# Weight sums one per slot, loaded two slots ahead, with their low parts on VectorE, in a fused attention and feed-forward kernel

## The chip, the cores and the metric

One core of a Trainium2 chip runs the whole program in one launch. The metric is the time of one execution on the device in microseconds. The engines named here are TensorE (PE in the profile), VectorE (DVE), ScalarE (ACT), GpSimd (POOL) and SyncE (SP), whose queue issues all the DMAs. Each engine runs its instructions in the order in which they are written, and engines wait for each other by semaphores.

## What is computed

The input x is 2 x 1024 x 512 in float32. A causal linear attention with 16 heads and its output projection are added to x, and then a gated feed-forward part:

```python
x = x + _layernorm(_L0_attn_ref(_layernorm(x), Wq, Wk, Wv, Wo))
x = x + _layernorm(_L0_ffn_ref(_layernorm(x), w_gate, w_up, w_down))

def _L0_ffn_ref(x, w_gate, w_up, w_down):
    h = silu(x @ w_gate) * (x @ w_up)      # 512 -> 2048
    h_sparse = _sparsify_2to4(h)           # of each 4 neighbours the 2 largest by size stay
    return h_sparse @ w_down               # 2048 -> 512
```

## The kernel before

Every large product is made of three fast multiplications. Each operand is split into a high part (ScalarE's cast to the short format fp32r) and a low part (the value less its high part), and high x high, low x high and high x low are added up in a bank. The profile shows the three as lines 784, 785 and 786. So every weight is loaded raw, cast by ScalarE, and its low part is made by another engine: in this kernel mostly GpSimd, whose helper `lo` is line 1906 for all of them.

The work is laid out in ticks. Attention takes slots a0 to a65. The feed-forward part takes slots f0 to f75; a slot here means one of these, `slot_f(n)`, of which each engine has its own. f0 stands between a64 and a65. Slots 0 to 31 handle the first batch row: slot n has a gate projection and an up projection of 12 multiplications each, and from slot 6 on one down projection of 12 for the hidden rows made earlier. From slot 32 on the second batch row is handled with fewer products, from sums of weight blocks (the manner of Strassen). For these the kernel makes, during slots 1 to 17, 16 **rounds of weight sums**, and keeps them in HBM (`s_keep`).

Round r goes through these steps:

- `load_sums(r)` on SyncE, line 595: two DMAs of 256 KB bring raw weights into one of four buffers of the tile `x_part`. It waits until the earlier round of that buffer is stored.
- `sum_weights(r)` on VectorE, lines 1642 to 1647: four additions or subtractions over 128x256 elements, in place, at the end of slot `SUM_AT[r]`.
- `split_sums(r)` on ScalarE, line 1285: the high part, 128x1024, into `x_hi`, in slot `SUM_AT[r] + 1`, behind ScalarE's weight splits of that slot (line 1187).
- `sum_low(r)` on GpSimd, line 1906 with `x_lo<-x_part`: the low part, 128x1024, over the raw sums, in slot `SUM_AT[r] + 1`, behind GpSimd's weight splits of that slot.
- `store_sums(r)` on SyncE, line 601: two DMAs of 512 KB, in slot `SUM_AT[r] + 2`.

Rounds 0 to 3 are loaded just before the feed-forward slots, the later ones at slot `max(SUM_AT[r-4] + 3, SUM_AT[r] - 2)`, at the end of what SyncE does in the slot. With the numbers of before, the store rule is the larger for most rounds: loads stand in SyncE's queue one slot ahead of their sum (round 4: load in slot 4, sum in slot 5). In front of them in a slot stand that slot's loads of `x_rows` (line 573), weight pieces (line 558, each waits until GpSimd has split the piece four before it), stores of split weights (`w_keep`, line 628) and stores of sums.

The rest of a slot that matters here:

- VectorE starts slot n with the gate product (line 1755: up projection of slot n-1 times its gated value). TensorE's up projection of slot n waits for that product of slot n-1 (`dve_h >= n - 1`). In slots with n % 4 == 3 comes the first comparison pair (lines 1602 to 1604), with n % 4 == 0 the second one and `keep_two` (lines 1609 to 1630), which masks four hidden rows. In every slot from 6 on one down projection is accumulated (1736, 1738). Behind these come variances of rows (1465) and last the sums.
- The masked rows are cast by ScalarE (1359). GpSimd makes the low parts of the first two (1906, `big_lo`) ahead of its weight splits of the slot, VectorE those of the other two at the start of the next slot (`first_lows`, 1635). The first down projection of these rows stands in TensorE's slot two later (6, 10, 14, 18, 22) behind the gate projection, and it needs all four low parts and the last split "down" weights of the unit, which are split in slot 4, 13, 21 and 29.
- From slot 19 on rows of the second batch row are turned (837) and split into `x_hi` and `x_lo`, over the buffers of the sums; ScalarE waits there until the stores of the sums have landed.

Of the kernel before, what the change touches and what calls it, by code (L numbers as in the profile page):

```python
# [8 lines left out]
ALU = mybir.AluOpType  # L9
ACT = mybir.ActivationFunctionType  # L10
F32 = mybir.dt.float32
# [24 lines left out]
ROUNDS = 4 * NU  # L36
# [12 lines left out]
def tick_f(n):  # L49
    return 65 if n == 0 else 66 + n  # L50
# [42 lines left out]

SUM_AT = [1, 2, 2, 3, 5, 6, 6, 7, 9, 10, 10, 11, 13, 14, 14, 15]


def sum_place(r):
    return 2 + r // 2 % 2, r % 2  # L100


def sum_buffer(r):
    half, a = sum_place(r)
    return 2 * (3 - half) + a
# [125 lines left out]
def pieces_at(tick, kinds):  # L231
    return [k for k, (piece, when) in enumerate(PLAN) if when == tick and piece[0] in kinds]
# [19 lines left out]
def build(nc, x, wq, wk, wv, wo, wg, wu, wd, cos_t, sin_t, causal, eye, x1, v_rest, s_keep, w_keep, out):  # L252
    with ExitStack() as ctx:
# [10 lines left out]
        def sem(name):  # L264
            return ctx.enter_context(nc.semaphore(name))
# [105 lines left out]
        def sum_raw(r):  # L371
            half, a = sum_place(r)
            return part[:, half, 2 * a:2 * a + 2, :]

        def sum_split(r):
            half, a = sum_place(r)
            return Xh[:, half, 2 * a:2 * a + 2, :], Xl[:, half, 2 * a:2 * a + 2, :]
# [96 lines left out]
        pe_g, pe_u, pe_d = sem("pe_g"), sem("pe_u"), sem("pe_d")  # L474
        ld_s = [sem(f"ld_s{i}") for i in range(4)]
        st_s = [sem(f"st_s{i}") for i in range(4)]
        dve_s1, dve_ss, act_ss, pool_ss = [sem(n) for n in ("dve_s1", "dve_ss", "act_ss", "pool_ss")]
        dve_t, act_t, pool_t = sem("dve_t"), sem("act_t"), sem("pool_t")
        ld_r = [sem(f"ld_r{i}") for i in range(RING)]
        st_k = [sem(f"st_k{i}") for i in range(8)]  # L480
# [67 lines left out]
        def _(sp):  # L548
            g = Gate(sp)
# [37 lines left out]
            def load_sums(r):  # L587
                k, up, buffer = r // 2, r % 2, sum_buffer(r)
                g.wait_ge(pe_q, 4 * STEPS)
                g.wait_ge(pe_k, STEPS)  # L590
                g.wait_ge(pe_v, B * TT)
                g.wait_ge(st_s[buffer], 32 * sum_uses(r))
                to = sum_raw(r).rearrange("p j (i c) -> p j i c", i=2)
                for i in range(2):
                    sp.dma_start(to[:, :, i, :], (wu if up else wg)[k // 2, 2 * (k % 2) + i].rearrange(
                        "p (j c) -> p j c", j=2)).then_inc(ld_s[buffer], 16)

            def store_sums(r):
                g.wait_ge(pool_ss, r + 1)
                for n, of in enumerate(sum_split(r)):  # L600
                    sp.dma_start(s_keep[r, n].rearrange("j p w -> p j w"), of.bitcast(F32)).then_inc(st_s[sum_buffer(r)], 16)

# [107 lines left out]
            for kind, i in TICKS:  # L710
# [44 lines left out]
                for r in range(4):  # L755
                    if tick == tick_f(0) - 2 + SUM_AT[r]:
                        load_sums(r)
                if kind == "f":
                    for r in range(ROUNDS):
                        if SUM_AT[r] + 2 == i:  # L760
                            store_sums(r)
                    for r in range(4, ROUNDS):
                        if max(SUM_AT[r - 4] + 3, SUM_AT[r] - 2) == i:
                            load_sums(r)
# [379 lines left out]
        def _(act):  # L1144
# [137 lines left out]
            def split_sums(r):  # L1282
                g.wait_ge(dve_ss, r + 1)
                g.wait_ge(st_s[sum_buffer(r)], 32 * sum_uses(r))
                copy(sum_split(r)[0], sum_raw(r)).then_inc(act_ss, 1)
# [47 lines left out]
            def slot_f(n):  # L1333
# [29 lines left out]
                for r in range(ROUNDS):  # L1363
                    if SUM_AT[r] + 1 == n:
                        split_sums(r)
# [82 lines left out]
        def _(dve):  # L1448
            g = Gate(dve)
# [188 lines left out]
            def sum_weights(r):  # L1638
                two, three = [sum_raw(r)[:, 0, half] for half in HALVES]
                four, one = [sum_raw(r)[:, 1, half] for half in HALVES]  # L1640
                g.wait_ge(ld_s[sum_buffer(r)], 32 * (sum_uses(r) + 1))
                dve.tensor_tensor(one, three, one, ALU.add).then_inc(dve_s1, 1)
                dve.tensor_tensor(three, two, three, ALU.subtract)
                g.wait_ge(dve_s1, 2 * r + 1)
                dve.tensor_tensor(two, one, two, ALU.subtract).then_inc(dve_s1, 1)
                g.wait_ge(dve_s1, 2 * r + 2)
                dve.tensor_tensor(four, four, two, ALU.subtract).then_inc(dve_ss, 1)

            def combine_x(step):
                high = [block[0].bitcast(F32) for block in (B11, B21, B12, B22)]  # L1650
                low = [block[1].bitcast(F32) for block in (B11, B21, B12, B22)]
                b11, b21, b12, b22 = range(4)
                if step == 0:
                    g.wait_ge(dve_xl, len(TURNS))
                    g.wait_ge(pe_u, EDGE - 4)
                if step == 6:
                    g.wait_ge(pool_wl, len(PLAN))
                g.wait_ge(dve_t, (0, 0, 1, 2, 3, 4, 5, 7, 8, 9)[step])
                to, first, other, op = ((raw_t1, high[b12], high[b11], ALU.subtract),
                                        (raw_t3, high[b22], high[b12], ALU.subtract),  # L1660
                                        (raw_t1, raw_t1, low[b12], ALU.add), (raw_t3, raw_t3, low[b22], ALU.add),
                                        (raw_t1, raw_t1, low[b11], ALU.subtract),
                                        (raw_t3, raw_t3, low[b12], ALU.subtract),
                                        (raw_t2, high[b22], raw_t1, ALU.subtract), (raw_t2, raw_t2, low[b22], ALU.add),
                                        (raw_t4, high[b21], raw_t2, ALU.subtract),
                                        (raw_t4, raw_t4, low[b21], ALU.add))[step]
                dve.tensor_tensor(to, first, other, op).then_inc(dve_t, 1)
# [77 lines left out]
            def slot_f(n):  # L1745
# [91 lines left out]
                for job in stats:  # L1837
                    variance(job)
                for r in range(ROUNDS):
                    if SUM_AT[r] == n:  # L1840
                        sum_weights(r)
                for step in {28: (0, 1), 29: (2, 3, 4), 30: (5, 6), 31: (7,)}.get(n, ()):
# [59 lines left out]
        def _(pool):  # L1902
            g = Gate(pool)

            def lo(dst, full, hi):
                return pool.tensor_tensor(dst, full, hi.bitcast(F32), ALU.subtract)  # L1906
# [47 lines left out]
                for job in at(tick, add_tick, ADDS):  # L1954
                    add(job)

            def sum_low(r):
                g.wait_ge(act_ss, r + 1)
                lo(sum_split(r)[1], sum_raw(r), sum_split(r)[0]).then_inc(pool_ss, 1)

            def t_low(n):
                to, of, count = ((T1, raw_t1, 7), (T3, raw_t3, 6), (T2, raw_t2, 8), (T4, raw_t4, 10))[n]
                g.wait_ge(act_t, n + 1)
# [13 lines left out]
            def slot_f(n):  # L1977
                tick = tick_f(n)
                for k in pieces_at(tick, "d"):
                    if not last_down(PLAN[k][0]):  # L1980
                        split(k)
                for job in at(tick, norm_tick, LATER):
                    scaling(job)
                if n == EDGE:
                    t_low(2)
                if n % 4 == 0 and 4 <= n <= EDGE:
                    d = n // 4 - 1
                    for i in range(2):
                        g.wait_ge(act_hh, 4 * d + i + 1)
                        lo(hidden(d)[1][:, i, :], hid[:, i, :], hidden(d)[0][:, i, :]).then_inc(pool_hl, 1)  # L1990
                for k in pieces_at(tick, "gud"):
                    if not last_down(PLAN[k][0]) and PLAN[k][0][0] == "d":
                        continue
                    split(k)
                for r in range(ROUNDS):
                    if SUM_AT[r] + 1 == n:
                        sum_low(r)
                if n in (30, 31):
                    t_low(n - 30)
                if n == EDGE + 2:  # L2000
                    t_low(3)
                if EDGE <= n < SLOTS:
                    k, beat = quad_of(n)
                    v, late = k // 2, k % 2
                    if beat == 1 and v:
                        hidden_lows(2 * (NU + v - 1) + late)
                if n == SLOTS:
                    hidden_lows(STEPS - 2)
                if n == SLOTS + 2:
                    hidden_lows(STEPS - 1)  # L2010
                for u in DOWN_AT:
                    for i in range(4):
                        if DOWN_AT[u][i] == n:
                            split_down(u, i)
                for job in at(tick, norm_tick, ENDING[:-1]):
                    scaling(job)
                for job in at(tick, norm_tick, ENDING[-1:]):
                    g.wait_ge(act_nm, len(SCALED) - 4)
                    deviation(job)
                for job in at(tick, add_tick, ADDS[:-4]):  # L2020
                    add(job)
# [69 lines left out]
```

## Time and profile before

| | us |
|---|---|
| median of 3 runs | 1245.32 (1244.94 to 1245.99) |
| profiled execution | 1244.29 |
| its span | 1242.5 |
| TensorE busy | 1185.8 (95%) |
| VectorE busy | 858.3 (69%) |
| ScalarE busy | 520.7 (42%) |
| GpSimd busy | 510.2 (41%) |

Busy is the time in which at least one instruction of the engine was running. A TensorE that is busy may still run at a lower clock; the page has a row for the clock that was granted. Feed-forward slots 1 to 21 take the time from about 663 to 877 us of the span. An idle time in square brackets behind a row is the one just before the instruction, with what ended it.

### The profile page before, as it was taken

To read this page: it belongs to the slowest core of one execution; us is meant where nothing else is said; L and a number is where in the kernel's file an instruction comes from. 1 tells how busy PE (TensorE), PEld (TensorE's weight loads), DVE (VectorE), ACT (ScalarE), POOL (GpSimd) and SP (SyncE) were. 2 spreads that over 40 slices of the span, in tenths; PEclk is the share of its full clock that TensorE was granted. 3 is DMA by queue.
4 is the path that set the end of the run, shared out by engine and by line. 5 is a ranking of instruction groups with operands and counts; after the bars stand their busy time and mean duration, and the time that the engine had idled before them with its cause. 6 is when DMAs were issued, how large, how long until landed. Compare 5 with 4: busy or idle time off the path is not lost.

```text
span 1242.5 us, 16278 instructions
## 1 busy us (share of the span) xinstructions
PE 1185.8 (95%) x5862; PEld 990.2 (80%) x5862; DVE 858.3 (69%) x1412; ACT 520.7 (42%) x1017; POOL 510.2 (41%) x397
## 2 busy tenths in 40 slices
PE   9999999999999999999999777799999999999987
PEld 7888888888888888888888565577787787888865
DVE  8845665666755466665656684876669869768698
ACT  4533544445444344454455232333432444334332
POOL 5512524425553143351555544554435633112124
PEclk9999999999999999999999998899999999999998
DMA  6321423314532233232365458456422565343411
GB/s 216 90 68 43 128 53 88 86 41 108 140 116 83 64 96 85 62 96 52 102 184 185 164 191 290 146 182 229 136 82 88 172 218 186 119 153 119 153 68 69
DMA packets 96368, 153.78 MB, mean 124 GB/s; under 512 B 10272, under 2 KB 31008, under 8 KB 96288
## 3 DMA queue, kind: packets, MB, share of 16 engines
q1 hardware_dynamic: 96288, 152.74, 39.5%
q8 instruction: 47, 0.77, 0.2%
q14 instruction: 33, 0.27, 0.1%
HBM read 96.60 MB, written 40.89 MB: 111 GB/s over the span
## 4 chain that ended last, share of the span: by engine, by line
PE 69%; DVE 16%; POOL 4%; issue 3%; DMA 3%; SPq 2%; ACT 2%; DVEq 0%; ACTq 0%; POOLq 0%
PE bank_q L786 7%; PE bank_q L784 7%; PE bank_q L785 7%; PE bank_y L786 5%; PE bank_y L785 5%; PE bank_y L784 5%; PE bank_od L1011 5%; PE bank_od L1014 4%; PE bank_t L784 3%; PE bank_t L786 2%; PE bank_t L785 2%; PE bank_s L908 2%; POOL big_lo L1906 2%; DMA x_part<-wu 2%; PE bank_s L784 2%
## 5 line engine op out<-in xcount | busy, mean ns | idle before, releaser
L784 PE MATMUL bank_q<-x_hi,w_hi 128*128 128x512 f32 x464 | 187.6, 404 | 0.5 <-ACT scratch L1313 0.4
L786 PE MATMUL bank_q<-x_lo,w_hi 128*128 128x512 f32 x464 | 182.7, 394 | 0.0
L785 PE MATMUL bank_q<-x_hi,w_lo 128*128 128x512 f32 x464 | 182.1, 393 | 0.0
L1906 POOL TENSOR_TENSOR w_lo<-stage,w_hi 128x512 fp32r<-128x512 f32 x60 | 78.6, 1319 | 127.0 <-ACT w_hi L1187 126.3
L1906 POOL TENSOR_TENSOR big_lo<-q_rows,big_hi 128x1024 fp32r<-128x1024 f32 x31 | 74.0, 2386 | 116.9 <-ACT big_hi L1226 116.9
L786 PEld LDWEIGHTS bank_q<-x_lo,w_hi 128*128 128x128 f32 x464 | 87.8, 189 | 19.2
L784 PEld LDWEIGHTS bank_q<-x_hi,w_hi 128*128 128x128 f32 x464 | 88.1, 190 | 18.6 <-ACT scratch L1313 1.5
L785 PEld LDWEIGHTS bank_q<-x_hi,w_lo 128*128 128x128 f32 x464 | 88.3, 190 | 16.8
L786 PE MATMUL bank_y<-wout_lo,a_hi 128*128 128x512 f32 x256 | 100.0, 391 | 0.0
L784 PE MATMUL bank_y<-wout_hi,a_hi 128*128 128x512 f32 x256 | 99.8, 390 | 0.0
L785 PE MATMUL bank_y<-wout_hi,a_lo 128*128 128x512 f32 x256 | 99.8, 390 | 0.0
L1906 POOL TENSOR_TENSOR big_lo<-hidden,big_hi 128x512 fp32r<-128x512 f32 x24 | 48.7, 2046 | 123.1 <-ACT big_hi L1359 75.6
L1011 PE MATMUL bank_od<-v_rows,scratch 128*128 128x130 f32 x512 | 95.1, 275 | 0.0
L1255 ACT ACTIVATE scratch<-bank_od,small 128x128 f32<-128x128 f32 x256 | 73.2, 373 | 42.2 <-DVE small L1555 42.2
L1014 PE MATMUL bank_od<-st_rows,q_rows 128*128 128x130 f32 x448 | 86.6, 275 | 0.0
L1267 ACT CAST a_hi<-bank_s 128x512 fp32r<-128x512 f32 x64 | 37.5, 586 | 111.0 <-PE bank_s L908 111.0
L1011 PEld LDWEIGHTS bank_od<-v_rows,scratch 128*128 128x128 f32 x512 | 79.1, 191 | 3.7
L1906 POOL TENSOR_TENSOR wout_lo<-stage,wout_hi 128x512 fp32r<-128x512 f32 x42 | 66.8, 1612 | 34.0 <-ACT wout_hi L1187 34.0
L1344 ACT ACTIVATE scratch<-hidden 128x512 f32<-128x512 f32 x32 | 20.3, 633 | 122.5 <-DVE hidden L1755 122.5
L1911 POOL TENSOR_TENSOR small<-small 128x1 f32<-128x1 f32 x64 | 38.4, 600 | 73.8 <-DVE small L1469 73.6
L1014 PEld LDWEIGHTS bank_od<-st_rows,q_rows 128*128 128x128 f32 x448 | 67.5, 190 | 0.0
L1587 DVE TENSOR_TENSOR a_lo<-bank_s,a_hi 128x512 fp32r<-128x512 f32 x64 | 44.2, 691 | 25.2 <-ACT a_hi L1267 25.1
(418 smaller groups left out, 3112.0 us busy)
## 6 DMA issues: line engine op xcount, KB each, us to landing
q_rows<-scratch SPq DMA_DIRECT2D x116, 128.0 KB, 2.3
x_rows<-x SPq DMA_DIRECT2D x48, 256.0 KB, 3.0
stage<-wq SPq DMA_DIRECT2D x32, 256.0 KB, 2.7
stage<-wo SPq DMA_DIRECT2D x32, 256.0 KB, 2.7
s_keep<-x_hi SPq DMA_DIRECT2D x16, 512.0 KB, 4.3
s_keep<-x_lo SPq DMA_DIRECT2D x16, 512.0 KB, 5.3
w_hi<-s_keep SPq DMA_DIRECT2D x32, 256.0 KB, 3.0
w_lo<-s_keep SPq DMA_DIRECT2D x32, 256.0 KB, 4.1
```

The source lines that it names most:

```text
L784: pe.matmul(ps, whi, xhi, start=first, stop=False, skip_group_check=True)
L785: pe.matmul(ps, wlo, xhi, start=False, stop=False, skip_group_check=True)
L786: return pe.matmul(ps, whi, xlo, start=False, stop=last, skip_group_check=True)
L908: ins = pe.transpose(psS[:, h * P:(h + 1) * P], Tn[:, h * P:(h + 1) * P], ident[:, :])
L1011: ins = pe.matmul(o, Sf[:, h * P:(h + 1) * P], Vr[:, c, :], start=True, stop=first, skip_group_check=True)
L1014: ins = pe.matmul(o, Q[:, (2 * p + h // 2) % 4, h % 2, t], St[:, :], start=False, stop=True, skip_group_check=True)
L1255: act.activation(Tn[:, h * P:(h + 1) * P], sums[:, h // 2, h % 2, 0:P], ACT.Identity, scale=share[:, h:h + 1]).then_inc(act_a, 1)
L1267: copy(Ah[:, :, :].rearrange("p h t -> p (h t)"), psS[:, :]).then_inc(act_ah, 1)
L1344: act.activation(ab[:, i, :], hid[:, i, :], ACT.Abs).then_inc(act_ab, 1)
L1587: dve.tensor_tensor(Al[:, :, :].rearrange("p h t -> p (h t)"), psS[:, :], Ah[:, :, :].rearrange("p h t -> p (h t)").bitcast(F32), ALU.subt ...
L1906: return pool.tensor_tensor(dst, full, hi.bitcast(F32), ALU.subtract)
L1911: pool.tensor_tensor(rstd[q % 4], mv[q % 4][:, 1:2], mhalf, ALU.pow).then_inc(pool_rs, 1)
```

## The change

`SUM_AT` becomes strictly increasing, one sum per slot, in slots 0 to 19 instead of 1 to 15. By the rule above, the loads of rounds 4 to 15 go to slots 3, 4, 5, 7, 8, 9, 11, 12, 13, 15, 16, 17: each two slots ahead of its sum. Round 0's load stands at tick a63 (was a64) and its sum in slot f0. The low part moves from GpSimd to VectorE, where it stands in slot `SUM_AT[r] + 1` ahead of that slot's own sum. The store waits for VectorE's semaphore.

```diff
-SUM_AT = [1, 2, 2, 3, 5, 6, 6, 7, 9, 10, 10, 11, 13, 14, 14, 15]
+SUM_AT = [0, 1, 2, 3, 5, 6, 7, 9, 10, 11, 13, 14, 15, 17, 18, 19]
...
             def store_sums(r):
-                g.wait_ge(pool_ss, r + 1)
+                g.wait_ge(dve_sl, r + 1)
...
+            def sum_low(r):
+                high, low = sum_split(r)
+                g.wait_ge(act_ss, r + 1)
+                dve.tensor_tensor(low, sum_raw(r), high.bitcast(F32), ALU.subtract).then_inc(dve_sl, 1)
...
                 for job in stats:
                     variance(job)
                 for r in range(ROUNDS):
+                    if SUM_AT[r] + 1 == n:
+                        sum_low(r)
+                for r in range(ROUNDS):
                     if SUM_AT[r] == n:
                         sum_weights(r)
...
-            def sum_low(r):
-                g.wait_ge(act_ss, r + 1)
-                lo(sum_split(r)[1], sum_raw(r), sum_split(r)[0]).then_inc(pool_ss, 1)
...
-                for r in range(ROUNDS):
-                    if SUM_AT[r] + 1 == n:
-                        sum_low(r)
```

## Rows read from the trace of the kernel before

**Rows 1.** Stretches: us, busy of PE, PEld, DVE, ACT, POOL (xcount), PEclk, DMA, GB/s.
```profile
663.00:880.00 217.00, 183.44 (x735) 144.13 (x734) 151.36 (x234) 73.83 (x120) 113.42 (x73) 0.91 0.59 199
880.00:960.00 80.00, 80.00 (x363) 65.97 (x362) 57.66 (x91) 28.28 (x48) 32.99 (x24) 1.00 0.33 109
...
765.00:772.00 7.00, 6.02 (x15) 4.80 (x16) 2.19 (x5) 2.57 (x4) 3.61 (x2) 0.54 1.00 338
```

**Rows 2.** Waits of TensorE, 663 to 880: us in total, times, longest.
```profile
PE bank_t L784 <- DVE hidden L1755: 11.7, 4, 5.8
PE bank_od L784 <- POOL big_lo L1906: 5.2, 2, 5.0
```

**Rows 3.** Waits of VectorE in the same stretch.
```profile
DVE x_part L1642 <- DMA x_part<-wg: 22.4, 2, 12.7
DVE x_part L1642 <- DMA x_part<-wu: 17.4, 5, 6.6
DVE small L1465 <- DMA x_rows<-x: 11.3, 2, 9.7
```

**Rows 4.** Chain of waits, 745 to 770: start us, us, what.
```profile
743.41 4.12 POOL big_lo L1906 x2
...
748.79 1.69 POOL u_lo L1906
...
757.14 1.33 SPq L595
...
765.15 6.08 DMA x_part<-wu
```

**Rows 5.** Instructions of tile x_part: duration ns min/median/max, first and last start.
```profile
L1906 POOL TENSOR_TENSOR x_lo<-x_part,x_hi x18: 2367/2570/2854, 678.7 to 958.8; 128x1024 fp32r<-128x1024 f32 x18
...
L1642 DVE TENSOR_TENSOR x_part<-x_part x16: 417/426/2527, 666.4 to 818.4; 128x256 f32<-128x256 f32 x16
...
L1643 DVE TENSOR_TENSOR x_part<-x_part x16: 412/420/2606, 667.8 to 818.8; 128x256 f32<-128x256 f32 x16
...
L1285 ACT CAST x_hi<-x_part x16: 1034/1042/1057, 672.7 to 837.1; 128x1024 fp32r<-128x1024 f32 x16
L1667 DVE TENSOR_TENSOR x_part<-x_part,x_lo x4: 1214/1216/2319, 945.2 to 952.0; 128x1024 f32<-128x1024 f32 x4
...
DMA to landing us min/median/max: 3.1/5.2/6.7
```

**Rows 6.** Tile x_part by stretch: us, busy of DVE, ACT, POOL, PEclk, DMA, GB/s.
```profile
663.00:880.00 217.00, 51.26 (x64) 16.31 (x16) 41.31 (x16) 0.91 0.59 199
```

**Rows 7.** VectorE in order of time: start us, us, line, operation, tiles.
```profile
699.97 0.69 DVE L1755 TENSOR_TENSOR hidden<-bank_q,scratch 128x512 f32<-128x512 f32 x1 [1.26 <-POOL big_lo L1906]
...
713.12 0.43 DVE L1642 TENSOR_TENSOR x_part<-x_part 128x256 f32<-128x256 f32 x1 [9.79 <-DMA x_part<-wg]
...
714.59 0.68 DVE L1755 TENSOR_TENSOR hidden<-bank_t,scratch 128x512 f32<-128x512 f32 x1
...
734.94 0.68 DVE L1755 TENSOR_TENSOR hidden<-bank_t,scratch 128x512 f32<-128x512 f32 x1
...
744.48 0.68 DVE L1630 TENSOR_TENSOR hidden<-hidden,scratch 128x512 f32<-128x512 f32 x1
746.43 0.69 DVE L1755 TENSOR_TENSOR hidden<-bank_q,scratch 128x512 f32<-128x512 f32 x1 [1.26 <-POOL big_lo L1906]
...
794.65 0.69 DVE L1755 TENSOR_TENSOR hidden<-bank_q,scratch 128x512 f32<-128x512 f32 x1 [1.26 <-POOL big_lo L1906]
...
836.82 0.69 DVE L1755 TENSOR_TENSOR hidden<-bank_q,scratch 128x512 f32<-128x512 f32 x1 [1.29 <-POOL big_lo L1906]
...
871.67 0.69 DVE L1755 TENSOR_TENSOR hidden<-bank_q,scratch 128x512 f32<-128x512 f32 x1 [0.26 <-POOL big_lo L1906]
```

**Rows 8.** ScalarE's high parts of rounds 4 and 7, in order of time.
```profile
717.36 1.04 ACT L1285 CAST x_hi<-x_part 128x1024 fp32r<-128x1024 f32 x1
...
746.76 1.04 ACT L1285 CAST x_hi<-x_part 128x1024 fp32r<-128x1024 f32 x1
```

More of the change, by code:

```diff
@@ L476, in build @@
         st_s = [sem(f"st_s{i}") for i in range(4)]
-        dve_s1, dve_ss, act_ss, pool_ss = [sem(n) for n in ("dve_s1", "dve_ss", "act_ss", "pool_ss")]
+        dve_s1, dve_ss, act_ss, dve_sl = [sem(n) for n in ("dve_s1", "dve_ss", "act_ss", "dve_sl")]
         dve_t, act_t, pool_t = sem("dve_t"), sem("act_t"), sem("pool_t")
```

## The prediction

> **What bounds the kernel now.** I read first the busy time by stretch. In the 217 us from 663 to 880 TensorE issued 735 multiplications at a granted clock of 0.91; in the 80 us after it, which run the same slots, 363 at 1.00 [rows 1]. At that later rate 735 need 162 us, so about 55 us of this stretch are lost, part as gaps and part as slow clock: in a piece right behind a long gap the granted clock reads 0.54 [rows 1]. The rest of the kernel is not touched by the change, except where a store of this stretch is waited for later. All rounds of weight sums lie in slots 1 to 17, which is this stretch.
>
> Next, who makes TensorE wait. There are two kinds, each the longest of its sort in [rows 2]: the "up" projection of slot n waits for VectorE's gate product of the slot before (line 1755, 11.7 us in 4 waits), and the first down projection of each group of four waits for the hidden rows' low parts (5.2 us in 2, and three more places of the kind). Both are VectorE running late: its in-order stream holds the masks in slots 4, 8, 12 and so on, the products, and the sums at the end of a slot. VectorE in turn waits 39.8 us for the raw weights that the sums read, in 7 waits of up to 12.7 us, and 11.3 us for rows of x [rows 3]. The third view, the chain of waits over slots 8 to 10, says why those loads are late [rows 4]: GpSimd's hidden low parts, then its weight splits, the sums' low part, then SyncE's stores, and only then the load at 757.1, landed 7 us later.
>
> Beside the waits VectorE is slowed. A sum operation over 128x256 takes 0.42 us at its least and median but up to 2.61 us [rows 5]; the long ones lie beside GpSimd's 128x1024 low part of 2.4 to 2.9 us. All 64 of them took 51.3 us, GpSimd's 16 low parts 41.3 [rows 6]. Undisturbed, a round passes in 1.5 us (from 713.12 to the next product at 714.59) [rows 7], 24 us in all. So some 27 us of VectorE are contention.
>
> The pace is read from VectorE's products that open slots 5, 9, 13, 17 and 21: 699.97, 746.43, 794.65, 836.82, 871.67 [rows 7]. The distances are 46.5, 48.2, 42.2 and 34.9 us, 171.7 together. Four slots of TensorE are 144 multiplications, 31.7 us at 363 per 80 us; some of these 363 are short transposes, so I take 32.7.
>
> **Part 1, sums one per slot, loads two slots ahead.** No round of work is added: 16 sums and 32 loads stay, spread over slots 0 to 19 in place of 1 to 15. A load now stands one slot earlier in SyncE's queue relative to its sum, so it has one slot (8 us) more; the worst wait was 12.7. I walk slot 8, the worst one. The last mask product ends at 745.2 (call it K) [rows 7]. In SyncE's queue of slot 8 come two weight loads which wait for GpSimd's splits behind the hidden low parts, then four stores of split weights, then the stores of the sums (one round now, two before), then load 8. It was issued at K+12.0 [rows 4]. With one round of stores less (2 DMAs; a DMA's issue took 1.33 us there [rows 4]) and without the sum's low part in GpSimd's queue (2.8 us, partly behind others) it goes at K+10 and lands at K+17. VectorE now wants it in slot 10, after its own slot 9, the low part and the product of slot 10, which I put at K+13.5 (wait for ScalarE 2.6, low part 1.2, slot 9's 4.7, slot 10's product and accumulation 1.2, wait 2.6, low part 1.2): a wait of 3.5 us where there were 12.7. Load 5, behind slot 4 where fewer commands stand, and loads 6 and 9 come out within 0 to 1 us of their sums; those of slots 3, 7, 11 to 13 land well ahead. So of 39.8 us some 5 stay (bounds 0 and 20, the latter if SyncE's queue is not relieved at all and each load in a quad's first slot is 6 us late). Round 0 now sums before the last attention slot's VectorE work; that stood idle for TensorE there, and it costs nothing unless the load issued some 5 us earlier lands over 2 us late.
>
> **Part 2, low parts from GpSimd to VectorE.** Removed from GpSimd: 16 operations of 2.58 us, 41.3 us [rows 6], and with them the 27 us of contention in the sums. Added to VectorE: 16 operations; the same shape, two inputs in SBUF, takes it 1.22 us at its least and median [rows 5], 19.5 us in all, all of it in the stream that sets the pace. The rows leave two prices open.
> The new wait: a low part waits for ScalarE's high part (1.04 us), and the next sum, the next slot's gate product and through it TensorE's next "up" stand behind it. In a mask slot the cast ended at 747.80, 2.6 us behind the last mask product; in another slot it began 2.8 us behind the gate product (714.59 to 717.36) [rows 7, 8] and ended at 3.8, of which the product and one accumulation cover 1.2, or 3.0 with the first comparisons. So a wait of 2.6, 2.6 and 0.8 us, 6 us per four slots; bounds 0 (GpSimd's and VectorE's other work hides it) and 9 (ScalarE late on weights).
> The contention that is left: GpSimd keeps the weight splits (one of 1.69 us stands in [rows 4]) and the hidden low parts (4.12 for a pair). I take 2.5 us per four slots, a split and a half met at its full length; bounds 0 and 8, four of its operations and more.
> What the trace shows of this contention is a VectorE operation of 0.42 us lasting 2.61 beside one of GpSimd. The Trainium skill, SBUF — State Buffer, section "SBUF: two separate sides", says the two share a port pair as an exclusive lock, held for the whole instruction, against VectorE operations with two SBUF inputs; the 2.61 agrees. Its Perfetto Trace Analysis, section "Optimizing Scalar/DVE Operations", draws from this that moving work between the two "might not help": that speaks against part 2 and is the third rival below.
>
> **The sum.** VectorE's work per four slots, undisturbed: from the gate product of a mask slot to the last mask product 10.2 us (734.94 to 745.2) [rows 7]; the other three slots' products, accumulations, comparisons and low parts 6.7 (eleven operations of 0.6); three sums 4.5; three low parts 3.6. That is 25. With 6 for ScalarE and 2.5 for contention: 33.5, close to TensorE's 32.7. The four distances become: slots 5 to 9, 33; 9 to 13, 37 (the 3.5 us wait of round 8); 13 to 17, 35; 17 to 21, 37 (a wait of up to 8 us for rows of x stays as the 11.3 of today, and low parts and sums of rounds 13 to 15 are new there). Together 142 against 171.7: 29.7. Before slot 5 the early sums, whose operations meet GpSimd's two low parts in slot 4, end about 4 us earlier (3 to 6). TensorE then regains another 1 us of clock. 34.5 us in all; the profiled run took 1244.3 (span 1242.5), the median is 1245.3, one more, and I add it: about 1210. Of the 55 us lost, 20 stay: a first down projection in slot 6 about 2 us late, slot 10 two, slot 14 six or seven (the last down weights are split behind the late gate product), slot 21 and 22 six, with clock after each. Errors of the walk, slot by slot, are worth 10 us either way: 1199 to 1220.
>
> **Rivals.**
> 1. The loads stay late: SyncE's queue waits as now for GpSimd's splits, the waits of mask slots stay, and the distances are 40, 40, 38 and 38 (today's less half the gain): 156 against 171.7 and 4 before, 1225. For it: the longest waits begin behind GpSimd, whose order keeps the splits behind the hidden low parts. Against: the extra slot.
> 2. TensorE alone sets the end: the ScalarE waits fall into slack, 5 us of loss stay, 1194.
> 3. The port makes the two engines one: what GpSimd stops doing VectorE does, and its sums still meet the remaining splits. Then only the load waits go (35) less 19.5 of low parts; 15 to 20 of these reach TensorE: about 1226. For it the 2.61 us; against it that one operation costs VectorE 1.22 and GpSimd 2.58, and that the largest GpSimd operations are those that go.
> 4. Slower: the queues close a ring. VectorE's low part waits for ScalarE's cast, which stands behind weight splits, whose loads stand in SyncE's queue behind the store that now waits for that low part. If the ring closes within one slot, a slot takes low part 1.2, store and load issue 2.5, landing 5.2 (to 6.7) [rows 5], split 0.6, cast 1.0 and wait 0.8: 11.3 to 12.8 us where the average now is 10.7 (171.7 over 16). That loses 10 to 33 us: 1265. It decides when a weight piece is loaded less than one slot before its split; the plan has most of them two slots ahead, and so I give it little.
> 5. One gain eats the other: VectorE loses in low parts and waits what it wins, 1245.
>
> **How the numbers follow.** Forecast 0.64, rival 1 0.12, rival 2 0.06, rival 3 0.10, rival 4 0.05, rival 5 0.03. The predicted time is the forecast's, 1210. From 1198 to 1226 lie the forecast with both errors and rivals 1 and 3; outside lie 2, 4 and 5. Faster by over 0.2% (about what a measurement can tell here) is 0.92, within it 0.03, slower 0.05.
>
> **What would show it.** The x_part waits of VectorE fall from 39.8 to about 5 us; the four sum operations have a mean near 0.45 us; sixteen x_lo operations of 1.2 to 2.5 us stand on VectorE, with about 25 us of waits for x_hi; TensorE's wait on line 1755 goes from 11.7 to under 2; the granted clock of the stretch is over 0.95; slot 21's product comes 33 us earlier, near 839. If that product comes as early but the end does not, something after slot 22 is wrong; if the low parts last 2.5 us each, rival 3 holds; if waits on x_hi are over 50 us, rival 4.

## The result, and the profile after

The changed kernel takes 1216.08 us (median of 4 runs, 1214.53 to 1218.87) against 1245.13 before in the same comparison; the ratio is 0.9771, with an interval of 0.9748 to 0.9794. By the ratio that is 28.5 us less (29.1 by the two medians, 27.1 in the spans of the two profiled executions, 1242.5 and 1215.4), where 35 were forecast.

The stretches of the changed kernel, with the columns of [rows 1]: the slots that took 217 us now take 190, and the 80 us behind them run as before.

```profile
663.00:853.00 190.00, 174.74 (x732) 141.15 (x731) 148.62 (x249) 73.88 (x121) 80.30 (x58) 0.95 0.65 219
853.00:933.00 80.00, 80.00 (x363) 65.99 (x362) 56.80 (x90) 27.59 (x48) 32.18 (x24) 1.00 0.37 122
```

At 363 per 80 us, 732 multiplications need 161 us, so 29 are lost where 55 were. The granted clock rose from 0.91 to 0.95. Next, who waits for whom in this stretch, first TensorE, then VectorE (rows 2 and 3 of before):

```profile
PE bank_st L837 <- DVE x_lo L1484: 7.3, 2, 4.5
PE bank_od L784 <- DVE big_lo L1635: 2.9, 3, 1.1
PE bank_od L784 <- issue: 2.5, 1, 2.5
PE bank_y L784 <- POOL wout_lo L1914: 2.3, 1, 2.3
```

```profile
DVE x_lo L1652 <- ACT x_hi L1285: 21.4, 12, 2.7
DVE small L1465 <- DMA x_rows<-x: 6.9, 1, 6.9
...
DVE x_part L1642 <- DMA x_part<-wg: 1.6, 1, 1.6
DVE x_part L1642 <- DMA x_part<-wu: 1.2, 1, 1.2
```

TensorE's wait for the gate product, 11.7 us in [rows 2], is gone. VectorE's wait for raw weights fell from 39.8 us [rows 3] to 2.8. The new wait for the high part is 21.4 us. What the operations of the sums cost VectorE, by line (busy us, mean ns, idle before and its cause); line 1652 is the low part that moved:

```profile
L1652 DVE TENSOR_TENSOR x_lo<-x_part,x_hi 128x1024 fp32r<-128x1024 f32 x16 | 26.3, 1641 | 21.4 <-ACT x_hi L1285 21.4
L1643 DVE TENSOR_TENSOR x_part<-x_part 128x256 f32<-128x256 f32 x16 | 11.0, 688 | 0.0
L1645 DVE TENSOR_TENSOR x_part<-x_part 128x256 f32<-128x256 f32 x16 | 9.9, 617 | 0.0
L1642 DVE TENSOR_TENSOR x_part<-x_part 128x256 f32<-128x256 f32 x16 | 9.7, 608 | 2.7 <-DMA x_part<-wg 1.6 <-DMA x_part<-wu 1.2
L1647 DVE TENSOR_TENSOR x_part<-x_part 128x256 f32<-128x256 f32 x16 | 7.7, 484 | 0.6
```

By the durations of their rows the four sum operations fell from 54 us to 38.3. Undisturbed, 64 operations of 0.42 us would be 27, so of 27 us of contention with GpSimd some 11 stay. And the pace, by the products that open slots 5, 9, 13, 17 and 21, as in [rows 7]:

```profile
698.83 0.68 DVE L1760 TENSOR_TENSOR hidden<-bank_q,scratch 128x512 f32<-128x512 f32 x1
...
734.48 0.68 DVE L1760 TENSOR_TENSOR hidden<-bank_q,scratch 128x512 f32<-128x512 f32 x1
...
768.08 0.68 DVE L1760 TENSOR_TENSOR hidden<-bank_q,scratch 128x512 f32<-128x512 f32 x1
...
805.75 0.68 DVE L1760 TENSOR_TENSOR hidden<-bank_q,scratch 128x512 f32<-128x512 f32 x1
...
844.78 0.68 DVE L1760 TENSOR_TENSOR hidden<-bank_q,scratch 128x512 f32<-128x512 f32 x1
```

The distances are 35.7, 33.6, 37.7 and 39.0 us: 146.0 together, where they were 171.7. Slot 21's product comes 26.9 us earlier, and so does all that follows. VectorE's own balance over just this part, slots 5 to 21, says what the 25.7 us are. The first fence is of before, the second of the changed kernel:

```profile
699.97:871.67 171.70, 145.26 (x572) 113.23 (x572) 115.57 (x180) 54.70 (x89) 85.73 (x52) 0.90 0.61 210
```

```profile
698.83:844.78 145.95, 134.84 (x568) 108.75 (x566) 115.36 (x193) 53.98 (x88) 58.20 (x39) 0.96 0.67 229
```

VectorE is as busy as it was, 115.6 and 115.4 us: what it won in contention it spent on the low parts. Its idle time fell from 56.1 to 30.6 us, by 25.5, and that is the gain. Within it the waits for raw weights fell by 34.4 us, from 37.2 to 2.8, and 14.7 us of waits for the high part are new. Which of the two parts of the change brought what can't be read from this balance; experiment 1 has them apart.

### The profile page after: what moved, and what is told of

It is laid out like the page before. It is cut to its first block, busy times and chain, and to the rows that moved or that the text cites. A ratio compares the mean times of both kernels' runs of the same rounds, so it can differ in the third digit from the quotient of the medians.

```text
span 1215.4 us, 16278 instructions
## 1 busy us (share of the span) xinstructions
PE 1176.5 (97%) x5862; PEld 986.5 (81%) x5862; DVE 857.9 (71%) x1428; ACT 521.0 (43%) x1017; POOL 476.1 (39%) x381
## 4 chain that ended last, share of the span: by engine, by line
PE 74%; DVE 14%; ACT 3%; issue 3%; POOL 3%; SPq 2%; DMA 2%; DVEq 0%; ACTq 0%
PE bank_q L784 8%; PE bank_q L786 8%; PE bank_q L785 8%; PE bank_y L784 5%; PE bank_y L786 5%; PE bank_y L785 5%; PE bank_od L1011 5%; PE bank_od L1014 4%; PE bank_t L784 3%; PE bank_t L786 3%; PE bank_t L785 3%; PE bank_s L908 2%; PE bank_s L784 2%; PE bank_s L785 2%; PE bank_s L786 2%
## 5 line engine op out<-in xcount | busy, mean ns | idle before, releaser
L1267 ACT CAST a_hi<-bank_s 128x512 fp32r<-128x512 f32 x64 | 37.6, 587 | 109.7 <-PE bank_s L908 109.7
L1919 POOL TENSOR_TENSOR small<-small 128x1 f32<-128x1 f32 x64 | 41.5, 648 | 75.3 <-DVE small L1469 74.9
```

The source lines that it names most:

```text
L1267: copy(Ah[:, :, :].rearrange("p h t -> p (h t)"), psS[:, :]).then_inc(act_ah, 1)
L1919: pool.tensor_tensor(rstd[q % 4], mv[q % 4][:, 1:2], mhalf, ALU.pow).then_inc(pool_rs, 1)
```

## The experiments

Every ratio below is to the kernel before, run on the same chip; the changed kernel's is 0.9771 (0.9748 to 0.9794). The kernels were run in four series, and two of different series are compared by these ratios.

**1. The two parts alone, and the lead of the loads.** The new slots with the low parts on GpSimd:

```diff
-SUM_AT = [1, 2, 2, 3, 5, 6, 6, 7, 9, 10, 10, 11, 13, 14, 14, 15]
+SUM_AT = [0, 1, 2, 3, 5, 6, 7, 9, 10, 11, 13, 14, 15, 17, 18, 19]
```

> Part 1 alone: the new slots of the sums and their loads, low parts on GpSimd as before. If the loads are the cause (my theory: of the gain of some 28 us, most comes from the load waits of 39.8 us): 1222 us (1216 to 1228), waits of VectorE for raw weights under 8 us. If the contention with GpSimd is the cause: most of the gain is lost, 1236 us (1230 to 1242), sum operations still at a mean of 0.8 us. If the low parts on VectorE cost as much as they save: equal to the changed kernel, 1216.

Measured: 1219.24 us, ratio 0.98 (0.9784 to 0.9816), 24.9 us less than before. Load waits are 8.1 us, and the contention is all there:

```profile
L1643 DVE TENSOR_TENSOR x_part<-x_part 128x256 f32<-128x256 f32 x16 | 18.7, 1167 | 0.0
```

The load theory holds: the schedule alone brings seven eighths of the gain, with sum operations that are even slower than before (57.6 us for the four lines, 54 before). VectorE's balance over slots 5 to 21 of this kernel:

```profile
697.51:845.19 147.68, 137.32 (x571) 110.28 (x572) 124.90 (x181) 53.72 (x88) 85.45 (x51) 0.95 0.67 226
```

Against it the changed kernel, which differs only in the low parts, is busy for 9.5 us less (115.4) and idle for 7.8 us more (30.6 where this one has 22.8), and takes 1.7 us less. So the busy time that did not change between the first and the last kernel hides two steps: the new slots raised it from 115.6 to 124.9, and moving the low parts brought it back.

The low parts on VectorE with the old slots, as an edit of the changed kernel:

```diff
-SUM_AT = [0, 1, 2, 3, 5, 6, 7, 9, 10, 11, 13, 14, 15, 17, 18, 19]
+SUM_AT = [1, 2, 2, 3, 5, 6, 6, 7, 9, 10, 10, 11, 13, 14, 14, 15]
```

> Part 2 alone: low parts on VectorE, the slots of the sums as before. Load theory: waits for raw weights stay at 25 us or more, 1236 us (1230 to 1243). Contention theory: the sum operations fall to a mean of 0.5 us and the time to 1222 (1216 to 1228). Third possibility: the low parts add 19.5 us and waits for the high part to a VectorE stream that still waits for loads, 1246 or more.

Measured: 1238.42 us, ratio 0.9957 (0.9941 to 0.9973), 5.4 us less. VectorE waits:

```profile
DVE x_part L1642 <- DMA x_part<-wg: 21.7, 4, 10.2
DVE x_lo L1652 <- ACT x_hi L1285: 20.2, 11, 3.6
...
DVE x_part L1642 <- DMA x_part<-wu: 4.6, 2, 2.5
```

The sum operations did fall, to a mean of 0.52 us, and the waits for raw weights from 39.8 to 26.3 us, though each load stands where it stood. The likely reason, not tested by itself, is that GpSimd's queue, on whose splits SyncE waits, has lost the sums' low parts. But 20.2 us of waits for the high part came in, and all this was worth little as long as the loads come late. The two parts alone add up to 30.3 us, the whole is 28.5: within the intervals they just add. Next, the changed kernel with each load one slot later:

```diff
                 for r in range(4):
-                    if tick == tick_f(0) - 2 + SUM_AT[r]:
+                    if tick == tick_f(0) - 1 + SUM_AT[r]:
                         load_sums(r)
...
-                        if max(SUM_AT[r - 4] + 3, SUM_AT[r] - 2) == i:
+                        if max(SUM_AT[r - 4] + 3, SUM_AT[r] - 1) == i:
```

> The changed kernel with every load one slot later in SyncE's queue, where it stands one slot ahead of its sum. If the second slot of lead is what removed the waits: waits for raw weights 15 to 30 us and 1224 us (1220 to 1232). If spreading the sums alone did it: waits under 8 us and 1216.

Measured: 1233.57 us, ratio 0.992 (0.9905 to 0.9935). The waits for raw weights are back:

```profile
DVE x_part L1642 <- DMA x_part<-wu: 16.7, 3, 7.4
DVE x_part L1642 <- DMA x_part<-wg: 15.3, 4, 7.3
```

So 18.5 of the 28.5 us hang on the second slot of lead, more than I expected. It is not the pure effect of rounds 4 to 15: rounds 0 to 3 are loaded a tick later too, and slot 1's product stands at 670.35 where it stood at 666.18, which is 4.2 us of it. Without the lead, sums one per slot and low parts on VectorE together bring 10, of which the low parts alone brought 5.4.

**2. What the sixteen low parts cost.** They are cut to one element of each 512, with waits, casts and DMAs kept. This kernel leaves out the low parts of the sums and stores the raw sums in their place:

```diff
-                for n, of in enumerate(sum_split(r)):
+                for n, of in enumerate((sum_split(r)[0], sum_raw(r))):
...
-                dve.tensor_tensor(low, sum_raw(r), high.bitcast(F32), ALU.subtract).then_inc(dve_sl, 1)
+                dve.tensor_tensor(sum_raw(r)[:, :, 0:1], sum_raw(r)[:, :, 0:1], high[:, :, 0:1].bitcast(F32), ALU.subtract).then_inc(dve_sl, 1)
```

> The changed kernel with the sums' low part cut to one element in 512 of each row half (the wait for ScalarE's high part, the place in the stream and all DMAs stay; the low parts of the sums are not computed, the raw sums are stored in their place). It prices the 16 operations on VectorE, whose times in the changed kernel add up to some 26 us. If VectorE's stream sets the pace through the sums: 5 to 10 us less, 1208. If only the first and last groups of four slots are bound by it: 2 to 4 less, 1213. If they lie in slack: 1216.

Measured: 1207.21 us, ratio 0.969 (0.9673 to 0.9708), about 10 us less than the changed kernel. The operations had 26.3 us together, and the cut ones still take 8.7, so of 17.6 us removed more than half reaches the end. TensorE's waits in the stretch:

```profile
PE bank_st L837 <- DVE x_lo L1484: 5.4, 2, 3.5
PE bank_y L784 <- POOL wout_lo L1914: 3.2, 1, 3.2
PE bank_od L784 <- DVE big_lo L1635: 1.4, 2, 0.8
```

With them cut, VectorE's product of slot 5 comes at 694.75 (698.83 in the changed kernel) and the distances are 32.6, 32.9, 37.6 and 38.1 us. TensorE in these four pieces:

```profile
694.75:727.37 32.62, 31.85 (x140) 25.99 (x140) 25.66 (x46) 14.42 (x24) 14.72 (x11) 1.00 0.73 250
727.37:760.30 32.93, 32.27 (x143) 26.35 (x142) 23.60 (x47) 10.78 (x17) 10.10 (x7) 1.00 0.82 279
760.30:797.88 37.58, 34.40 (x140) 27.77 (x139) 26.08 (x47) 15.15 (x25) 14.82 (x11) 0.91 0.54 182
797.88:835.99 38.11, 34.16 (x154) 27.59 (x152) 26.81 (x59) 13.84 (x22) 13.08 (x13) 1.00 0.71 242
```

In the first two groups it is busy for all but 1.4 us at the full clock, so TensorE sets the pace. In the third it waits 3.2 us for the last down weights in slot 14, and the granted clock is 0.91. In the fourth it has 154 multiplications to issue, 11 to 14 more than in the others, and is idle for 3.9 us, in the two waits for split rows.

**3. The waits for the high part.** Three ways to cover them. First, in the slots with a sum, the low part behind it:

```diff
                 for r in range(ROUNDS):
-                    if SUM_AT[r] + 1 == n:
-                        sum_low(r)
-                for r in range(ROUNDS):
                     if SUM_AT[r] == n:
                         sum_weights(r)
+                for r in range(ROUNDS):
+                    if SUM_AT[r] + 1 == n:
+                        sum_low(r)
```

> The changed kernel with the low part behind the slot's own sum instead of ahead of it, so that in most slots the wait for ScalarE's high part (21.4 us in 12 waits) is covered by a sum of 1.5 us. If these waits are on the path: they fall to 8 to 12 us and the time by 2 to 5, 1212. If they lie in slack, or the mask slots, which have no sum, hold what matters: 1216 within 1.5.

Measured: 1214.76 us, ratio 0.9765 (0.9747 to 0.9782). The waits fell from 21.4 to 9.8 us as expected, the time by nothing that can be told; load waits rose to 11.6 us, and the five low parts of the mask slots have no sum to stand behind. Second, ScalarE's cast for the sums ahead of its weight splits:

```diff
+                for r in range(ROUNDS):
+                    if SUM_AT[r] + 1 == n:
+                        split_sums(r)
                 for k in pieces_at(tick, "gud"):
                     if PLAN[k][0][0] != "d" or last_down(PLAN[k][0]):
                         split(k)
-                for r in range(ROUNDS):
-                    if SUM_AT[r] + 1 == n:
-                        split_sums(r)
```

> The changed kernel with ScalarE's high part of the sums ahead of its weight splits of the slot. VectorE's wait for high parts falls from 21.4 to about 12 us (two casts of 0.5 us fewer in front). If that wait is on the path: 2 to 4 us less. Against it: GpSimd's weight splits, and SyncE's loads behind them, come 1 us later in each slot, and the last down weights too, which TensorE waited 2.3 us for in slot 14: then 1216 or 1 to 2 us more.

Measured: 1219.05 us, ratio 0.9786 (0.9768 to 0.9804). The waits fell to 15.0 us, and TensorE's wait for the last down weights in slot 14 rose from 2.3 to 4.0. It gains nothing, and may lose 2 us. Third, only the mask slots' low parts, moved behind the next slot's product and hidden low parts:

```diff
                 if n % 4 == 1 and 4 < n < EDGE:
                     first_lows(n // 4 - 1)
+                    for r in range(ROUNDS):
+                        if SUM_AT[r] + 2 == n:
+                            sum_low(r)
...
                 for r in range(ROUNDS):
-                    if SUM_AT[r] + 1 == n:
+                    if SUM_AT[r] + 1 == n and n % 4:
                         sum_low(r)
```

> The changed kernel with the five low parts that fall into mask slots (rounds 3, 6, 9, 12, 15) moved behind the next slot's gate product and hidden low parts, so that nothing of the hidden rows waits for them and for ScalarE (2.2 to 2.7 us of wait and 1.3 to 2.1 of work each). If these five, not all sixteen, are what the low parts cost: TensorE's gaps in slots 6, 10 and 14 shrink by 2 to 4 us each, 1208 (1205 to 1211), as good as with no low parts at all (1207). If the amount of VectorE's work counts, not its place: 1215.

Measured: 1211.67 us, ratio 0.9745 (0.9729 to 0.9761). TensorE's waits in the stretch:

```profile
PE bank_y L784 <- POOL wout_lo L1917: 4.6, 1, 4.6
PE bank_st L837 <- DVE x_lo L1484: 4.1, 2, 2.7
PE bank_od L784 <- issue: 2.5, 1, 2.5
```

By ratio this is some 3 us better than the changed kernel, though the two intervals overlap, so that it is likely and not shown; it is a third of what cutting all sixteen brings. Five operations out of sixteen explain a third, not all, of the cost: the expectation of 1208 was too good. The gap of slot 14 grew, since the last down weights are split late anyway.

**4. Slots 19 to 22, the largest loss left.** In the changed kernel VectorE waits 6.9 us for rows of x in slot 18 (the load is issued at 814.27, behind the stores and loads of the sums), ScalarE waits 4.29 us in slot 20 until the store of round 13 has landed, whose buffer it writes over, and TensorE waits twice for the split rows. Rows of ScalarE and then TensorE in order of time:

```profile
831.37 0.59 ACT L1158 CAST x_hi<-bank_st 128x512 fp32r<-128x512 f32 x1 [4.29 <-DMA s_keep<-x_lo]
```

```profile
832.82 0.63 PE L837 MATMUL bank_st<-ident,x_rows 128*128 128x128 f32 x4 [2.80 <-DVE x_lo L1484]
846.20 1.09 PE L837 MATMUL bank_st<-ident,x_rows 128*128 128x128 f32 x4 [4.54 <-DVE x_lo L1484]
```

Three row loads one slot earlier:

```diff
-                for job in at(tick, lambda j: stat_tick(j) - (1 if j in TURNS else 0), ROWS):
+                for job in at(tick, lambda j: stat_tick(j) - (1 if j in TURNS else 0) - (j in (('mid', 1, 0), ('mid', 1, 1), ('mid', 1, 2))), ROWS):
                     load_rows(job)
```

> The changed kernel with the loads of the first three row tiles of the second batch row one slot earlier in SyncE's queue, ahead of the stores and loads of the sums that stood in front of them. If the 6.9 us wait of VectorE for rows in slot 18 is what makes TensorE wait 7.3 us in slots 20 and 21 for the split rows: that wait falls under 2, the 7.3 under 3, and the time by 4 to 8: 1210. If the store of round 13 or the low parts set it: 1216 within 1.5.

Measured: 1217.88 us, ratio 0.9772 (0.975 to 0.9793), the same. VectorE no longer waits for rows, but ScalarE's wait for the store grew from 4.3 to 7.2 us:

```profile
ACT x_hi L1158 <- DMA s_keep<-x_lo: 7.2, 1, 7.2
```

In both kernels this cast of ScalarE begins at 831.4: it came to its place sooner and waited longer for the same store. My theory of the row load falls: with one wait removed the next stands in its place. With the early rows, the stores of slots 19 to 21 ahead of the row loads, which wait for TensorE:

```diff
+                if kind == "f":
+                    for r in range(ROUNDS):
+                        if SUM_AT[r] + 2 == i and i >= 19:
+                            store_sums(r)
                 for job in at(tick, lambda j: stat_tick(j) - (1 if j in TURNS else 0) - (j in (('mid', 1, 0), ('mid', 1, 1), ('mid', 1, 2))), ROWS):
                     load_rows(job)
...
-                        if SUM_AT[r] + 2 == i:
+                        if SUM_AT[r] + 2 == i and i < 19:
                             store_sums(r)
```

> The kernel with early row loads, and from slot 19 on the stores of the sums ahead of the row loads, which wait for TensorE's turn of an earlier tile. ScalarE's wait of 4.3 us for the store of round 13 falls under 1. If that wait is on the path: 1 to 3 us less than early row loads alone. If it is covered: the same within 1.5.

Measured: 1214.97 us, ratio 0.9753 (0.9732 to 0.9774); ScalarE still waits 5.9 us for the store. By ratio this is 2.4 us less than the early rows alone, within the intervals, so a gain isn't shown. The edit barely moved the store of round 13: its second DMA is issued at 824.17, where it was 824.48 with the early rows and 823.64 in the changed kernel. The order in SyncE's queue is not what makes it late. Then the rounds themselves sooner:

```diff
-SUM_AT = [0, 1, 2, 3, 5, 6, 7, 9, 10, 11, 13, 14, 15, 17, 18, 19]
+SUM_AT = [0, 1, 2, 3, 5, 6, 7, 9, 10, 11, 13, 14, 15, 16, 17, 18]
```

> The changed kernel with rounds 13, 14 and 15 summed in slots 16, 17 and 18 (17, 18 and 19 in the changed one), so that round 13 is stored a slot before the second batch row's first tile is split over its buffer. If the store of round 13, and the row load behind the sums' DMAs, are together what holds slots 20 to 22: ScalarE's wait for s_keep (4.3, and 7.2 with early rows) goes, TensorE's wait for x_lo falls from 7.3 to under 3, and the time by 3 to 6: 1211. If VectorE's amount of work in slots 16 to 20 sets it: the wait moves to slots 17 and 18, 1216 within 1.5.

Measured: 1215.11 us, ratio 0.9767 (0.9753 to 0.9782). ScalarE's wait for the store is gone and TensorE's wait for the rows falls from 7.3 to 3.9 us, but the distance from slot 13 to 17 grows from 37.7 to 41.3 us, where a fourth sum now stands, behind the masks, and the one from 17 to 21 falls from 39.0 to 34.6. The four together are 144.9 us, 1.0 less than in the changed kernel. This fits the second theory of the expectation, that VectorE's amount of work in these slots is what counts: a wait taken away there returns as another.

**5. Combinations.** The mask slots' low parts later, low parts behind the sum, and the sooner rounds:

> Both edits of this series, and in the other slots the low part behind the slot's sum. If the two causes are separate the gains add: 1204 (1200 to 1208). If one limit stands behind both: as the better of the two.

Measured: 1215.3 us, ratio 0.9771 (0.9756 to 0.9785): the gains do not add, they vanish. VectorE's waits for raw weights are back at 19.8 us, and TensorE waits 3.7 us for a gate product again. Without the sooner rounds:

> The kernel with the mask slots' low parts moved behind the next gate product, and in the other slots the low part behind the slot's own sum; the rounds in the slots of the changed kernel. It is the last combination without the sooner rounds, which brought load waits of 19.8 us back. If those loads were what cost the combination its gain: 1210 (1208 to 1213), with waits for raw weights under 12 us and TensorE's longest gap in slot 14. If the low part behind the sum is what cost it: 1214 or more.

Measured: 1212.87 us, ratio 0.9729 (0.971 to 0.9748), 13.0 us of load waits, a little over the 12 expected. It was the sooner rounds that cost the combination its gain. By ratio this is the best kernel of the study that computes everything, 33.7 us less than before and about 5 less than the changed one; whether it beats the kernel with the mask slots' low parts later (0.9745) can't be told from these intervals.

## Why the prediction came out as it did

The time, 1216, lies inside the range, and the side was right; 6 us of the forecast gain are missing (the sum itself gives 1210.8, written as about 1210). In the profiled spans, 4.0 of them are missing in the four distances, 2.9 before slot 5, and 0.8 behind slot 21, where 1 us of clock was forecast and 0.2 came.

- **Part 1, the load waits: right.** About 5 us were to stay of 39.8; 2.8 did. The walk of slot 8 put the issue of its load at K+10, where K is the last mask product's end. In the changed kernel K is 729.8 and the row of SyncE's queue is this one, K+9.7:

```profile
739.56 2.70 SPq L595 DMA_DIRECT2D x_part<-wg  x2
```

  Its sum began at 746.1 after a wait of 1.6 us, at K+16.3 (forecast K+17, with 3.5).
- **Part 2, the wait for the high part: put too large.** 6 us per four slots were put in, 24 in slots 5 to 21. Of the 21.4 us measured 6.7 lie before slot 5; the 14.7 behind it are 3.7 per four slots: 6.0, 3.2, 4.9 and 0.6 in the four groups. The waits in the mask slots were 0.6 to 2.7.
- **Part 2, the contention left: too small.** I took 2.5 us per four slots, 10 in all. Over their undisturbed durations (0.42, 1.22, and 1.28 for a pair of hidden low parts) the sums of slots 5 to 21 had 6.4 us more, the low parts 6.7 and VectorE's own hidden low parts 2.7: 15.8 in all. The low parts themselves, two inputs in SBUF as the sums, last up to 2.2 us beside the hidden low parts and splits that stay on GpSimd.
- **The four distances: 4 us short, by errors that offset.** They were to be 33, 37, 35 and 37, together 142: 100 of undisturbed work of VectorE, 24 for the high part, 10 of contention and 8 of other waits. They were 35.7, 33.6, 37.7 and 39.0, together 146.0: some 99.6 of work, 14.7, 15.8, and 15.9 of other waits, of which rows of x are 6.9 and raw weights 2.8. The 9 us too many in the first term paid for most of what the last two lacked; that the sum came out within 4 us is in part luck.
- **Before slot 5: the term furthest off for its size.** It said 4 us earlier (3 to 6); slot 5's product came 1.1 us earlier. The term was made from the sums alone. The low parts of rounds 0 to 3 and their four waits, which the sum of the later slots had, were left out of it: the changed kernel waits 6.7 us there for the high part and has four low parts of 1.2. Cutting the low parts to nothing brought 4.1 us back in this place. The first down projection therefore still waits: slot 6 loses some 6.5 us, 3.9 in gaps and the rest in slow clock behind them, where 2 and a little clock were put.
- **What stays lost:** 20 us were forecast, 29 by the count of multiplications (some 24 if the gaps and the slow multiplications are added). Slots 6, 10 and 14 lost some 6.5, 3.5 and 4 us with their slow clock, where 2, 2 and 6 to 7 were put. Slots 20 to 22 lost 10 where 6 were: the walk had the late rows of x, but not that ScalarE waits for the store of round 13.
- **The rivals.** That the loads stay late is what the kernel with one slot of lead shows, at 1233.6. That the port makes the two engines one did not hold for the time: moving the low parts cost nothing and gained some 3 to 5 us. The doubt that the Trainium skill raises in Perfetto Trace Analysis, section "Optimizing Scalar/DVE Operations", that offloading between GpSimd and VectorE might not help, is borne out in part. With the old slots the move left VectorE's busy time over slots 5 to 21 nearly as it was (115.6 and 114.1 us); with the new ones it lowered it by 9.5 us, of which 7.8 came back as idle time. No run showed the ring of queues.

The pace rule behind the forecast, that a slot takes the longer of TensorE's 8.2 us and VectorE's own stream with its waits, held in the first half of the stretch, where cutting the low parts brings 32.6 and 32.9. In the last two groups, which did not go below 37 in that kernel, the rule lacks what TensorE itself loses: the wait for the last down weights and the slow clock behind it in the third, the turning of rows and the waits for them in the fourth. Why the split rows are late is not settled: neither the load of the rows nor the store alone explains it.

## What to carry to other kernels

Count the slots between a load's issue and its use in the queue in which it stands, not in time: here the second slot of lead was worth 14 to 18 us, in a queue that stops once per four slots for GpSimd's split of a weight piece (14.4, 10.4, 13.4 and 10.6 us in the changed kernel). Where a step moves onto the engine that sets the pace, look at what stands right behind it: the five low parts between the masks and the next product seem to cost as much each as the average of all sixteen, and could be moved past that product at no loss. And before a wait is removed, look who waits next in the same slot: in slots 18 to 20 the rows of x, the store and VectorE's own work took turns, and none of three edits there brought a gain that can be told.

## What the runs showed of the hardware

A VectorE operation with two inputs in SBUF that starts behind a GpSimd one lasted about as long as GpSimd's, without any idle time that the profile would show: 0.42 us became up to 2.6 beside a 128x1024 operation of GpSimd (2.57 us), and up to 1.5 beside its 128x512 operations (1.3 to 1.5 us) in the changed kernel. Where VectorE's started first, GpSimd's was the one that grew: the low part at 743.33 kept 1.23 us, and the 128x512 operation that GpSimd began at 743.89 took 1.82. The gate product, which reads one input from a bank, kept 0.68 to 0.69 us in every place of both kernels.
